# Block-diagonal keys of a windowed attention, written by 36 eight-row transfers per unit instead of nine stack transfers and twelve mask products

## The reference, cut to what matters

```
x = x + attention(layernorm(x))
    q, k, v = split(xw @ w_qkv.T + b_qkv)             # per window of 49 tokens, 12 heads x 8 channels
    attn = q @ k.T / sqrt(8) + bias + shift_mask      # 12 matrices of 49 x 49 per window
    o = softmax(attn) @ v ;  o @ w_proj.T + b_proj
t = t + experts(layernorm(t))                         # 4 experts, 96 -> 384 -> 96, top 2 by a softmax gate
```

## Time and profile before

| | |
|---|---|
| median of 3 runs | 7468.48 us (7466.52 to 7471.74) |
| span of the profiled execution | 7472.1 us |
| PE busy | 7129.8 us (95%) |
| DVE busy | 5951.8 us (80%) |
| ACT busy | 4441.6 us (59%) |
| POOL busy | 2691.2 us (36%) |

### The profile page before, as it was taken

One profiled execution on the slowest core, in us unless ns is written; L12 is line 12 of the kernel. 1 busy time (PEld: TensorE's weight loads), 2 busy tenths in 40 slices (PEclk: granted clock), 3 DMA queues, 4 the chain that ended last, 5 costly groups with the idle time before them and its releaser, 6 DMA issues.

```text
span 7472.1 us, 236413 instructions
## 1 busy us (share of the span) xinstructions
PE 7129.8 (95%) x87040; PEld 5658.9 (76%) x87040; DVE 5951.8 (80%) x17441; ACT 4441.6 (59%) x8959; POOL 2691.2 (36%) x1799
## 2 busy tenths in 40 slices
PE   5999999999999999999999999999999999999998
PEld 4777777777777777777777777777777777777777
DVE  6788778888788887878787788787888778887886
ACT  4566655665566655656565566655665566655664
POOL 3333333333333333333333333333333333333332
PEclk9999999999999999999999999999999999999999
DMA  1111111111111111111111111111111111111110
GB/s 49 35 32 35 33 34 32 34 34 34 32 34 35 33 33 34 34 33 34 33 34 33 34 32 34 33 34 32 35 33 34 32 34 35 34 32 34 34 33 18
DMA packets 168131, 250.97 MB, mean 34 GB/s; under 512 B 44272, under 2 KB 129008, under 8 KB 166768
## 3 DMA queue, kind: packets, MB, share of 16 engines
q1 hardware_dynamic: 166896, 234.60, 11.0%
HBM read 80.28 MB, written 38.54 MB: 16 GB/s over the span
## 4 chain that ended last, share of the span: by engine, by line
PE 52%; issue 27%; POOL 13%; DVE 4%; ACT 2%; SPq 1%; POOLq 0%; DMA 0%; DVEq 0%
PE ps_f L1010 18%; PE ps_t L926 10%; PE ps_o L945 7%; PE ps_s L916 4%; POOL rstd L399 4%; POOL rstd L383 3%; PE ps_f L954 3%; PE ps_f L1007 3%; PE ps_s L907 3%; ACT pt_sb L498 2%; POOL xn L393 2%; POOL xn L388 2%; POOL p_sb L417 2%; PE ps_f L865 1%; DVE stat L691 1%
## 5 line engine op out<-in xcount | busy, mean ns | idle before, releaser
L417 POOL TENSOR_TENSOR p_sb<-p_sb,s_rec 113x588 f32<-113x588 f32 x1024 | 1213.6, 1185 | 3244.9 <-DVE s_rec L677 3244.9
L1010 PE MATMUL ps_f<-w_sb,g_sb 128*112 128x96 f32 x18432 | 1963.7, 261 | 0.0
L1010 PEld LDWEIGHTS ps_f<-w_sb,g_sb 128*112 128x112 f32 x18432 | 1916.3, 178 | 0.0
L483 ACT ACTIVATE g_sb<-ps_f 128x392 f32<-128x392 f32 x3072 | 1524.3, 497 | 287.8 <-PE ps_f L859 217.7
L494 ACT ACTIVATE p_sb<-s_sub 113x588 f32<-113x588 f32 x1024 | 723.3, 706 | 1612.2 <-DVE s_sub L665 1612.2
L857 PE MATMUL ps_f<-x_hi,w_hi 128*128 128x392 f16 x3072 | 1040.7, 339 | 117.7 <-issue 103.5
L663 DVE TENSOR_REDUCE s_max<-ps_s 113x12 f32<-113x588 f32 x1024 | 770.8, 753 | 412.1 <-PE ps_s L916 405.6
L858 PE MATMUL ps_f<-x_lo,w_hi 128*128 128x392 f16 x3072 | 1038.3, 338 | 0.0
L859 PE MATMUL ps_f<-x_hi,w_lo 128*128 128x392 f16 x3072 | 1036.9, 338 | 0.0
L675 DVE TENSOR_REDUCE s_sum<-p_sb 113x12 f32<-113x588 f32 x1024 | 779.5, 761 | 199.7 <-ACT p_sb L494 161.9
L926 PE MATMUL ps_t<-ident,p_sb 113*113 113x113 f32 x6144 | 854.3, 275 | 49.9 <-POOL p_sb L417 49.9
(11 more groups left out here) (114 smaller groups left out, 10867.8 us busy)
## 6 DMA issues: line engine op xcount, KB each, us to landing
k_st<-qk_hi SPq DMA_DIRECT2D x768, 49.0 KB, 2.0
q_st<-qk_hi SPq DMA_DIRECT2D x768, 49.0 KB, 2.0
xr<-x SPq DMA_DIRECT2D x224, 139.1 KB
out<-xr SPq DMA_DIRECT2D x224, 139.1 KB
xa<-x SPq DMA_DIRECT2D x224, 136.5 KB
k_st<-qk_lo SPq DMA_DIRECT2D x384, 49.0 KB, 2.0
q_st<-qk_lo SPq DMA_DIRECT2D x384, 49.0 KB, 2.0
xa<-x SPq DMA_DIRECT2D x224, 10.5 KB
```

Source lines behind the costliest of these rows:

```text
L417: nc.gpsimd.tensor_tensor(p, p, s_rec[:, :].unsqueeze(2).broadcast_to([SPAN, HEADS, WW]), ALU.mult).then_inc(pnorm_done, 1)
L483: nc.scalar.activation(g_sb[:, chunk, half * STRIP:(half + 1) * STRIP], h_bank[k % 3][:, 0:STRIP], ACT.Gelu, scale=1.0 / WSCALE).then_inc( ...
L1010: ins = T.matmul(y[:, k * C:(k + 1) * C], g_sb[:, e * CPE + c, j * LANES:(j + 1) * LANES], w2_sb[:, e * CPE + c, :], start=False, stop=(c ...
```

## The change

`build_stacks(b)` no longer writes `k_st`, which is gone. Instead 36 transfers of eight rows x 784 float16 (12.5 KB each) write the heads' rows straight to their places in `k_bd`: 3 parts x 3 groups x 4 heads. The rows that must be zero are zeroed once at the start and never written. The 24 transfers that read `qk_hi` wait for the two high pieces of the keys alone, the 12 that read `qk_lo` wait for the low ones. The nine query transfers stay, behind them on the same queue. `spread_keys`, its 12 products and its semaphore are gone from VectorE. TensorE waits for the 36 transfers by `k_in`. Since it no longer waits for VectorE there, a wait for the second step of `router_a` is put ahead of `scores(a, 0)`.

SyncE's row in the first unit of the loop, before: behind the `xa` loads come the wait and the nine key transfers, a register step and the query transfers. In these rows `x2` means two alike in a row.

The core of the diff:

```diff
             def build_stacks(unit):
-                for kind, stack, parts, landed in ((1, k_st, (qk_hi, qk_lo, qk_hi), k_in),
-                                                   (0, q_st, (qk_hi, qk_hi, qk_lo), q_in)):
-
-                    sp.wait_ge(qkhi_done, at(unit, N_QK, 4 - 2 * kind))
-                    sp.wait_ge(qklo_done, at(unit, N_QK, 4 - 2 * kind))
-                    for g in range(GROUPS):
-                        for r, part in enumerate(parts):
-                            sp.dma_start(stack[32 * r:32 * r + 32, g, :],
-                                         part[32 * g:32 * g + 32, kind, :]).then_inc(landed, 16)
+                sp.wait_ge(qkhi_done, at(unit, N_QK, 2))
+                for r in (0, 2):
+                    spread_part(r, qk_hi)
+                sp.wait_ge(qklo_done, at(unit, N_QK, 2))
+                spread_part(1, qk_lo)
+
+                sp.wait_ge(qkhi_done, at(unit, N_QK, 4))
+                sp.wait_ge(qklo_done, at(unit, N_QK, 4))
+                for g in range(GROUPS):
+                    for r, part in enumerate((qk_hi, qk_hi, qk_lo)):
+                        sp.dma_start(q_st[32 * r:32 * r + 32, g, :],
+                                     part[32 * g:32 * g + 32, 0, :]).then_inc(q_in, 16)
...
+            def spread_part(r, part):
+
+                for g in range(GROUPS):
+                    for j in range(GH):
+                        src = 32 * g + HD * j
+                        dst = 32 * r + HD * j
+                        sp.dma_start(k_bd[dst:dst + HD, g, j, :], part[src:src + HD, 1, :]).then_inc(k_in, 16)
...
-            def spread_keys(a):
-
-                dve.wait_ge(k_in, at(a, N_STACK, N_STACK))
-                for g in range(GROUPS):
-                    for j in range(GH):
-                        V.tensor_scalar(k_bd[0:C, g, j, :], k_st[:, g, :], head_rows[:, j:j + 1], None,
-                                        ALU.mult).then_inc(kbd_done, 1)
...
             def step(f, a, b, u):
-                if a is not None:
-                    spread_keys(a)
                 router_b(f)
...
                     pe.wait_ge(q_in, at(a, N_STACK, N_STACK))
-                    pe.wait_ge(kbd_done, at(a, N_KBD, N_KBD))
+                    pe.wait_ge(k_in, at(a, N_SPREAD, N_SPREAD))
...
                 if a is not None:
+                    pe.wait_ge(router, at(f, N_ROUTER, 2))
                     scores(a, 0)
```

More of the change, by code:

```diff
@@ L120 @@
 N_STACK = 16 * 3 * GROUPS
-N_KBD = GROUPS * GH
+N_SPREAD = 16 * 3 * GROUPS * GH
 QSCALE = HD ** -0.5
@@ L189, in build @@
         q_st = sb("q_st", [128, GROUPS, TOK], F16)
-        k_st = sb("k_st", [C, GROUPS, TOK], F16)
         k_bd = sb("k_bd", [128, GROUPS, GH, TOK], F16)
@@ L238, in build @@
         rstd1_done, centre1_done, norm1_done = sem("rstd1_done"), sem("centre1_done"), sem("norm1_done")
-        x1lo_done, qklo_done, kbd_done = sem("x1lo_done"), sem("qklo_done"), sem("kbd_done")
+        x1lo_done, qklo_done = sem("x1lo_done"), sem("qklo_done")
         q_in, k_in = sem("q_in"), sem("k_in")
@@ L806, in prologue @@
                     qk_low((0, 0), t)
-                spread_keys((0, 0))
                 softmax_pair((0, 0), 0)
```

## The result

The changed kernel takes 8699.6 us (8681.5 to 8728.0, 4 runs) against 7468.5 us: 1.165 times as long, 95% interval 1.163 to 1.167. I had forecast 7935 and a range up to 8600. It is slower, by the mechanism that was forecast, and by 2.6 times the forecast amount (1231 us for 467).

A forecast was written before the change was run, and what follows sets the result against it. TensorE, busy 95% of the span, was taken to bound the kernel. 7472.1 + 456 (plain units) + 12 (first unit) = 7940 us for the profiled execution, 7935 beside the median, 6.2% slower; range 7470 to 8600.

The forecast's parts named there:

- the price of an eight-row issue: SyncE's time to issue one eight-row key transfer between two places in SBUF: taken as 0.40 us.
- three readings: Excess of a 32-row issue over 0.25 us goes with engines (0.42 or 0.36), rows (0.33), or any SBUF-to-SBUF transfer (0.53 to 0.59).
- my upper bound: An eight-row issue costs at most 0.59 us, the price of the same kind of transfer with four times the rows.
- The chain: From TensorE's start of scores to the next, through SyncE's issues: 41.4 + 36 (i + 0.10) us, i being one issue; 59.4 at 0.40.
- my term for them: Plain units, without the loop's jump: TensorE waits 3.2 us and loses 1.6 to clock, 4.8 in 95 units: 456 us.
- the turns: The 31 units with the loop's jump: TensorE's own pause covers the transfers, 59.4 being under 61.7 us, so 0.
- The clock: After TensorE's 3.2 us wait in a plain unit the granted clock falls, costing 1.6 us more.
- The factor four fifths: Loss of clock at TensorE, 2.0 us, taken in four units of five, since 3.2 us is a little short: 1.6.
- The removal: Taking 12 products, 4.09 us a unit, off VectorE is worth 0, since `router_b` needs `gexp`, late at the same time.
- faster: Transfers hidden and TensorE's clock back sooner at the loop's jump, 19 us less 8: 7458 us; chance 0.03.
- The first unit: At the start TensorE has no cover, so nine key issues (5.7 us) become 18.0: 12 us.
- the flat rival: SyncE's issue from SBUF to SBUF costs 0.53 to 0.59 us whatever its rows: 8650 us with 0.55; chance 0.24.

The follow-up runs named there:

- The probe: The kernel before plus 184 more transfers of 16 kinds, issued by SyncE after all of its work; one execution took 7593 us.
- The runs with 18: The changed kernel with 18 of the 36 key transfers, two heads of four in each group: 7494.5 us, 1.0038.
- 24: The changed kernel with 24 of the 36 key transfers, two groups of three: 7628.8 us, 1.0223.
- the run with 27 transfers: The changed kernel with 27 of the 36 key transfers, three heads of four: 7897.9 us, 1.0572.
- the detour through HBM: The changed kernel with keys stored whole to HBM scratch by two transfers and loaded back by 12, in place of 36: 7486.8 us, 1.0026.

## Why the prediction was wrong

**The step that failed is the price of an eight-row issue.** I took 0.40 us; it is 0.625. The rows had left three readings, and I chose the middle by the number of engines, since the packets differed there. The probe shows that neither engines nor rows carry the excess, but the two ends in SBUF: one row costs 0.589 there, 32 rows 0.590. The row that should have weighed more was in hand: between 4 and 52 rows the issues with HBM differ by 0.06 only the earlier trace rows, so a reading by which 24 rows fewer save 0.19 had nothing beside it. The price even lies 0.034 above my upper bound, which had been drawn at 0.591 on the tacit assumption that fewer rows cannot cost more.

**The chain was right.** It put the point from which TensorE waits at 36 x 0.41 = 14.8 us of issues. The runs with 18 (12.1 us of issues, no wait), 24 (16.1, 0.9 us) and 27 (18.2, 2.8) show it at some 15.3. With 0.625 the sum as I had written it would have given 41.4 + 36 x 0.725 + 2.0 = 69.5 us a unit and 8990 in all. Measured are 67.0 from one start of the scores to the next. Of the 2.5 us between them 1.7 are in the 36 issues, 24.4 in place of 26.1, mostly because I put the drawing out at 0.06 an issue by the 32-row rows and it is 0.02. Another 0.4 are in the query stage and its landing (7.1 in place of 7.5), and 0.4 in the stretch up to the last high keys, where the clock costs 1.6 in place of 2.0.

A check on the rest of the sum is the run with 27 transfers. Its issues take 18.2 us, where I had forecast 18.0, and it takes 7898 us, where I had forecast 7935. That it comes so near has some luck in it: the plain units come out under my term for them, 361 us in place of 456, and the turns, which I had put at 0, add 54.

**The clock** was sized well: 1.6 us a unit forecast for a wait of about 3, 1.6 measured with 27 transfers at 2.8; 2.0 for longer ones, 2.2 of TensorE's busy time measured. The factor four fifths behind the 1.6 had been a judgement, so that it fits so well is luck in part. My remark that the turns hide the transfers up to 61.7 us holds for the transfers: with 24 and with 27 of them TensorE waits for none at a turn. It does not hold for the clock that the wait before has cost.

**The removal was worth nothing**, as forecast, with `gexp` last in its place, though not at the same time: it ends 0.84 us earlier, which nobody waits for. I had not seen what is lost at the ends of the images. My case *faster*, that fewer instructions on VectorE bring the clock back sooner at the turns, did not come: the units with a turn became 0.35 us longer.

**The first unit**: 12 us forecast, 18 by the flat rival; 27 measured up to the second unit's first maximum, 19 of them in the first unit and 8 in the second, which has less cover than the later ones.

**The rival that came true** is the flat price, given 8650 for 0.55 us, with a chance of 0.24. Beside it stood a rule of the Trainium skill (DMA: Bandwidth & Descriptors, Rules for kernel authors), that under 64 KB a transfer is mostly overhead. The runs agree for transfers between two places in SBUF, where eight rows of 196 bytes and of 1568 bytes cost 0.62 us alike to issue. They agree less with an end in HBM, where in a row of issues eight rows cost 0.30 and 32 rows 0.42.

The Trainium skill (DMA: Bandwidth & Descriptors, Issuing engines are not separate DMA queues) also states that the time to initiate a transfer is usually small beside the transfer. Here it is 0.6 us beside 2.0 to landing for one transfer, but some 30 us for 45 in a row, since issues add up on their queue and landings overlap.

## What to carry to other kernels

Count the issues that stand between the data and the first transfer that somebody waits for, multiply by what one issue of the same kind (same two memories) takes, and compare that with the cover; neither bytes nor rows take the place of the count. When a transfer must move small pieces between partitions, try the detour through HBM: here an eight-row issue cost half, one transfer gathered pieces from three places, and the 2.7 us from the first store to the first load were paid once a unit. Work that is taken from an engine which waits soon after for a third one gives nothing, so look first at what it would wait for. When a small loss is left over, look through the list of waits for a line that the kernel before does not have, ahead of guessing at the clock.

## What the runs showed of the hardware

- An issue on SyncE's queue from SBUF to SBUF takes 0.58 to 0.63 us for one to 128 rows and 0.2 to 1.6 KB a row; with one end in HBM it takes 0.30 for eight rows and, behind another issue of its kind, 0.42 to 0.43 for 32 and 128. The first of such a row takes 0.31 to 0.36, and a single store of 96 rows 0.32.
- Between two places in SBUF eight rows take 0.625 us, and 1, 4, 16 and 32 rows 0.584 to 0.590.
- The exponentials on GpSimd (`gexp`, 112 x 28) take 5.62 us beside VectorE's float16 products and 4.78 without them, in all the runs that leave the products out. In the kernel before they take 4.8 to 5.0 in the units with a turn, where at most 0.6 us of the products run beside them.
- In the profiled execution with TensorE waits of 0.9 us the granted clock fell no more often than before (34 times), and its matmuls took 0.2 us more a unit; with waits of 2.8 us it fell 108 times and they took 1.6 more, with 9.0 (3.8 at a turn) 158 times and 2.2 more.
- A jump back in the loop costs TensorE 5.7 us: 3.4 of standing still, and the rest behind it, where the granted clock is 0.50 for a while. With 14 jumps in place of 30 the same work took 1.2% less.
